# Moving the q and v steps of a blocked factorisation between its leaves, and the clearing of a tile behind one of them

## The chip, the cores and the metric

The kernel runs on one core of a Trainium2 chip. The metric is the time of one execution on the device in microseconds; the median of three runs of the kernel before is 1110.0 us (1108.01, 1110.0 and 1110.34).

## What is computed

A block of three layers on x of shape (8, 1024, 256), float32: half of a feed-forward with ternary weights, then an attention-like recurrence, then half of the same feed-forward. The recurrence is this, for each of 8 batches over 1024 tokens:

```
Q, K, V = x Wq' + bq, x Wk' + bk, x Wv' + bv          # H = 128
A = I, M = 0
for each token:  s = k.q ;  u = k / (|k| + eps)
                 Au = A u ;  denom = 1 + u.Au ;  A -= Au Au' / denom
                 M += v (s Au / denom)' ;  o = M q
```

The kernel does it in chunks of 128 tokens: 64 pairs of a chunk and a batch, each with a 128x128 matrix that is factorised. Q, V and the product of u and q (the s of every token) are needed only later.

## The kernel before, in words

Three phases follow each other, with a barrier of all engines between them: the first feed-forward with the keys; the **first factorisation**; and a third phase with a second factorisation, the outputs and the second feed-forward. The change touches the first factorisation alone (about 332 to 538.5 us in the trace). It gives the inverse factor T of every one of the 64 matrices, in the SBUF tile `T` of 128 x 64 x 128, and it makes q, v and u.q beside that.

The factorisation goes in four blocks of 32 rows, r = 0 to 3. VectorE's work of a block is `take(r)` (L1009, a transpose of the diagonal blocks out of PSUM), `leaf(r)` (L1018, L1021, L1033 and L1036: 32 dependent elimination steps on all 64 matrices at once) and `turn(r)` (L1046, L1047: transposes that publish the result on the semaphore `turned`). TensorE then does `finish_diagonal(r + 1)` in two halves of 128 matmuls of 32x32 each (L1268, then L1275); between them VectorE's `over_d(r)` (L1059) and ScalarE's `next_block(r)` copy what the second half reads. The second half lets `take(r + 1)` start. I call the stretch from the start of `turn(r)` to the start of `take(r + 1)` the turn-over r.

While VectorE is in leaf r, the other engines have the work that `beside(r)` lists: TensorE the products `done(r)` (L1195), `panel(r)` (L1202, L1215) and `diagonal(r + 1)` (L1202, L1255), ScalarE their copies, and between those the **steps of q and v**, sixteen in all (n = 0 to 15). A step is `qv(n)` on TensorE (L1286 for q, L1293 for v) and on ScalarE (L1152 and a copy), and on SyncE's DMA queue `store_q(n)` (L910), `load(n + 2)` (L897, the input tile of step n + 2, which may be asked for when TensorE is through with step n) and `store_v(n)` (L915). `QV_OF` says which steps go beside which leaf: 5, 4, 2 and 5.

u.q: `load_u(r)` (L905) brings the u of the steps of leaf r, VectorE multiplies them with q in `times_q(r)` behind `turn(r)` (L1078; at most three of them ahead of `over_d(r)`, the others behind it), and TensorE sums them in `dots(r)` (L1303), at the start of what it does beside leaf r + 1. `load_u(r)` waits for `dots(r - 1)`, since it reuses the buffers.

SyncE runs all DMAs of the phase on one queue, in program order: the weights, load(0), load(1), load_u(0), then **three DMAs that clear T's columns above the diagonal blocks** (L954: from zeros in `ident`, rows of 384, 256 and 128 bytes), and then for each r `keep_d` (L921), `load_u(r)`, `keep_rows(r - 1)` (L937, the finished rows into T) and the stores and loads of the steps of r.

TensorE waits in `qv(n)` until the input tile has landed (`a_in`), and it does `finish_diagonal(r + 1)` only when the steps beside leaf r are through, since they stand ahead of it in its program.

Of the kernel before, what the change touches and what calls it, by code (L numbers as in the profile page):

```python
# [32 lines left out]
NW = P // W  # L33
# [675 lines left out]

QV_OF = [range(0, 5), range(5, 9), range(9, 11), range(11, 16)]
QV_MAX = max(len(x) for x in QV_OF)

# [16 lines left out]
def factorise(nc, ctx, name, m, c, a=None):  # L732
# [16 lines left out]
    def sem(what):  # L749
        return ctx.enter_context(nc.semaphore(f"{name}_{what}"))  # L750
# [54 lines left out]
    if first:  # L805
        w_in = sem("wqv_in")
        a_in = [sem(f"aT_in{s}") for s in range(2)]
        u_in = sem("uT_in")
# [4 lines left out]
        uq_done = sem("uq_done")  # L813
        dots_done = sem("dots_done")
# [5 lines left out]
    def block_of(r):  # L820
        return slice(W * r, W * r + W)

    def rows_of(q):
        return slice(W * q, W * q + W)
# [7 lines left out]
    def after(r):  # L832

        return slice(W * (r + 1), P)
# [3 lines left out]
    def fills_of(r):  # L838
        out = []
        if r > 0:  # L840
            if first or r < NW - 1:
                out.append("done")
            if not first:
                out.append("done right")
        if r < NW:
            if first or r < NW - 1:
                out.append("panel")
            if not first:
                out.append("panel right")
        return out  # L850
# [32 lines left out]
    def slot(n):  # L883

        return next(n - x[0] for x in QV_OF if n in x)

    def beside(r):

        return zip_longest(fills_of(r), QV_OF[r] if first and r < NW else ())  # L890

    def sync(sp):
        def load(n):
            s = n % 2
            if n > 1:
                sp.wait_ge(v_made, n - 1)
            sp.dma_start(aT[s][:], m.aT[n]).then_inc(a_in[s], 16)  # L897

        def load_u(r):
            if r:  # L900

                sp.wait_ge(dots_done, r)
            for n in QV_OF[r]:
                half = slice(HC * (n % 2), HC * (n % 2) + HC)
                sp.dma_start(uT[:, slot(n)], uT_v[n // 2, :, half]).then_inc(u_in, 16)  # L905

        def store_q(n):
            half = slice(HC * (n % 2), HC * (n % 2) + HC)
            sp.wait_ge(q_done, n + 1)
            sp.dma_start(qT_v[n // 2, :, half], qT[:, slot(n)]).then_inc(q_stored, 16)  # L910

        def store_v(n):
            s = n % 2
            sp.wait_ge(v_done, n + 1)
            sp.dma_start(v_v[n // 2, :, HC * s:HC * s + HC], v_out[s][:]).then_inc(v_stored[s], 16)  # L915

        def keep_d(r):

            sp.wait_ge(turned, r + 1)
            for q in range(4):  # L920
                sp.dma_start(m.dinv[block_of(r), NQ * q:NQ * (q + 1)], dT[r][rows_of(q), 0:NQ]  # L921
                             ).then_inc(stored, 16)

        def keep_rows(r):

            what = "done" if first else "done right"
            sp.wait_ge(emptied, fill_number[r + 1, what] + 1)
            if r == NW - 1:
                sp.wait_ge(half_emptied, 1)
            if not first:  # L930

                sp.wait_ge(filled, fill_number[NW - 1, "panel right"] + 1)
            for q in range(4):
                pairs = slice(NQ * q, NQ * (q + 1))
                if first:
                    cols = slice(0, W * (r + 1))
                    sp.dma_start(m.T[block_of(r), pairs, cols], Y[r][rows_of(q), :, cols]  # L937
                                 ).then_inc(stored, 16)
                else:
                    sp.dma_start(m.W[block_of(r), pairs], YR[r][rows_of(q)]  # L940
                                 ).then_inc(e.rows_in[q] if r == NW - 1 else stored, 16)

        if first:
            w_v = a["WqkvT"].rearrange("(c p) n -> p c n", p=P)
            for i in range(2):
                sp.dma_start(wqv[:, :, i], w_v[:, :, 2 * i * H:(2 * i + 1) * H]).then_inc(w_in, 16)
            sp.dma_start(bq[:], a["bqkv"][0:H].rearrange("(p o) -> p o", o=1)).then_inc(w_in, 16)
            load(0)
            load(1)
            load_u(0)  # L950
            for i in range(NW - 1):

                zeros = c.ident[block_of(i), after(i)]
                sp.dma_start(m.T[block_of(i), :, after(i)],  # L954
                             zeros.unsqueeze(1).to_broadcast([W, NP, P - W * (i + 1)])).then_inc(stored, 16)

        def fetch_q():

            sp.wait_ge(diag_done, NW - 1)
            for g in range(4):  # L960
                pairs = slice(NQ * g, NQ * (g + 1))
                sp.dma_start(m.KK[:, pairs], m.qT[pairs].rearrange("n i j -> i n j")).then_inc(stored, 16)

        for r in range(NW + 1):
            if r:
                keep_d(r - 1)
                if first and r < NW:
                    load_u(r)
            if r == NW and e.early is not None:
                e.early(sp)  # L970
            if first and r:
                keep_rows(r - 1)
            if not first and r == NW - 1:
                fetch_q()
                for k in range(NW - 1):
                    keep_rows(k)
            if not first and r == NW:
                keep_rows(r - 1)
            if first and r < NW:
                for n in QV_OF[r]:  # L980
                    store_q(n)
                    if n + 2 < NSTEP:
                        load(n + 2)
                    store_v(n)
        if first:
            sp.wait_ge(q_stored, 16 * NSTEP)
            for s in range(2):
                sp.wait_ge(v_stored[s], 16 * NSTEP // 2)
        if e.early is None:
            sp.wait_ge(stored, e.all_stored)  # L990
            if not first:
                for q in range(4):
                    sp.wait_ge(e.rows_in[q], 16)

    def vector(v):
# [76 lines left out]

        def times_q(r, which):

            v.wait_ge(u_in, 16 * (QV_OF[r][-1] + 1))
            for n in which:
                v.wait_ge(q_done, n + 1)
                nc.vector.tensor_tensor(uT[:, slot(n)], uT[:, slot(n)], qT[:, slot(n)], ALU.mult  # L1078
                                        ).then_inc(uq_done, 1)

        for r in range(NW):
            take(r)
            leaf(r)
            turn(r)
            if r < NW - 1:
                if first:
                    times_q(r, QV_OF[r][:3])
                over_d(r)
                if first:
                    times_q(r, QV_OF[r][3:])  # L1090
            elif first:
                times_q(r, QV_OF[r])
        empty_half()

    def scalar(act):
        def copy(dst, src):
            return nc.scalar.activation(dst, src, ACT.Copy)
# [58 lines left out]
            copy(v_out[s][:], ps_v[:]).then_inc(v_done, 1)  # L1156

        def keep_dots():
            act.wait_ge(dots_done, NW)
            copy(dots_rows[:], ps_dots[0:NP, 0]).then_inc(rows_kept, 1)  # L1160
            act.wait_ge(rows_turned, 1)
            copy(m.uq[:], ps_dots[:, 1, 0:NP])
# [6 lines left out]
        for r in range(NW + 1):  # L1169
            if 0 < r < NW - 1:  # L1170
                act.wait_ge(turned, r)
                nc.scalar.mul(nd[:], dT[r - 1][:, 0:NQ], -1.0).then_inc(nd_done, 1)
                act.wait_ge(nd_done, r)
            for what, n in beside(r):
                if what is not None:
                    empty(r, what)
                if first and r == NW:
                    keep_dots()
                if n is not None:
                    qv(n)  # L1180
            if r < NW - 1:
                reset(r + 1)
                next_block(r)

    def tensor(pe):
# [110 lines left out]

        def dots(r):

            pe.wait_ge(uq_done, QV_OF[r][-1] + 1)
            for n in QV_OF[r]:  # L1300
                for j in range(HC):
                    at = n * HC + j
                    i = nc.tensor.matmul(ps_dots[0:NP, 0], c.ones_at[:, NP - 1 - at:2 * NP - 1 - at],  # L1303
                                         uT[:, slot(n), j], start=(at == 0), stop=(at == NP - 1))
            i.then_inc(dots_done, 1)
# [34 lines left out]
    if not first:  # L1340
        e.works, e.panels, e.Z, e.ZR, e.M, e.Tt = works, panels, Z, ZR, M, Tt
        e.inject_units = inject_units
    e.emptied, e.half_emptied, e.all_emptied = emptied, half_emptied, len(fill_list)
    e.sync, e.vector, e.scalar, e.tensor = sync, vector, scalar, tensor
    return e

# [660 lines left out]
```

## Time and profile before

| | |
|---|---|
| median of three runs | 1110.0 us |
| profiled execution, its own time | 1110.93 us |
| its span | 1109.2 us |
| TensorE busy | 933.6 us, 84% |
| VectorE busy | 798.4 us, 72% |
| ScalarE busy | 532.2 us, 48% |
| first factorisation, from take(0) to the start of the third phase | 334.1 to 538.5 us |
| mean DMA traffic | 103 GB/s |

The profile is of one execution. The page gives the busy time of each engine; the trace behind it gives every instruction with its start, its duration and what the engine waited for. A group of instructions is written as line, engine, operation, output and inputs, with how many there are; a square bracket gives the engine's idle time ahead of it and what ended it. "issue" in such a bracket means that nothing in the profile explains the wait. Rows marked PEld are weight loads, which stand ahead of each matmul.

### The profile page before, as it was taken

The page shows a single profiled execution, that of the slowest core. Times are in us where ns is not written, and L with a number is a line of the kernel's source. Part 1 is how long each engine was busy: PE and PEld are TensorE (multiplying, and loading weights), DVE is VectorE, ACT ScalarE, POOL GpSimd, SP SyncE. Part 2 cuts the span into 40 slices and gives each one's busy share as a digit, 9 for nine tenths or more (in the row PEclk, how much of TensorE's full clock was granted, in tenths as well). Part 3 has the DMA queues.
Part 4 walks back from the last instruction along what each step waited for, and adds up shares of the span by engine and source line. Part 5 has one row for each costly group of instructions (what it writes and reads, how often), then busy time and mean ns, then how long its engine had stood idle before and what let it go on. Part 6 is the DMA issues. An engine that isn't in the chain of part 4 may idle for free.

```text
span 1109.2 us, 28575 instructions
## 1 busy us (share of the span) xinstructions
PE 933.6 (84%) x11691; PEld 720.0 (65%) x11691; DVE 798.4 (72%) x2553; ACT 532.2 (48%) x1093; POOL 301.1 (27%) x256
## 2 busy tenths in 40 slices
PE   4799999999976796677899446692799999999998
PEld 1467777777763675565797425582667777777766
DVE  6878787877648898978359797886366666566663
ACT  4678787787741142112226212101165666556574
POOL 4355353535210000000000000000674554546340
PEclk9999999999997797889899776896899999999999
DMA  5353546455239452344443000056532433424231
GB/s 151 70 127 101 154 114 145 118 140 132 86 126 228 116 152 71 98 117 116 106 131 107 4 2 4 4 155 150 156 87 77 105 96 80 121 67 105 57 77 57
DMA packets 185522, 113.98 MB, mean 103 GB/s; under 512 B 85808, under 2 KB 178352, under 8 KB 184752
## 3 DMA queue, kind: packets, MB, share of 16 engines
q1 hardware_dynamic: 168496, 95.38, 33.9%
q10 hardware_dynamic: 16896, 16.78, 4.8%
q8 instruction: 92, 1.51, 0.6%
q14 instruction: 38, 0.31, 0.1%
HBM read 49.16 MB, written 37.75 MB: 78 GB/s over the span
## 4 chain that ended last, share of the span: by engine, by line
PE 33%; DVE 15%; issue 2%; POOL 1%; ACT 1%; DMA 0%; DVEq 0%; POOLq 0%; SPq 0%
PE ldl_work L1875 10%; PE ldl_work L1863 10%; DVE ldl_lane_matrix L1036 6%; DVE ldl_rank_one L1033 4%; DVE lane_rows L1018 2%; PE ldl_work L1847 2%; DVE ldl_lane_dinv L1021 2%; PE ldl_work L1439 2%; PE ldl_work L1449 1%; PE ldl_work L1817 1%; PE ldl_work L1830 1%; PE ldl_work L1831 1%; PE ldl_work L1838 1%; PE ldl_work L1195 1%; PE ldl_work L1811 1%
## 5 line engine op out<-in xcount | busy, mean ns | idle before, releaser
L1625 POOL TENSOR_TENSOR T<-T,out_bv_rows 128x512 f32<-128x512 f32 x16 | 20.4, 1272 | 453.9 <-DVE out_s_over_d L1728 448.0
L387 DVE TENSOR_TENSOR ffn_h_rest<-ffn_ps_h,ffn_h_high 128x512 f16<-128x512 f32 x128 | 87.2, 686 | 53.7 <-ACT ffn_ps_h L557 53.2
L556 ACT ACTIVATE ffn_h_high<-ffn_ps_h,b_columns 128x512 f16<-128x512 f32 x128 | 87.9, 686 | 65.4 <-PE ffn_ps_h L630 64.8
L1875 PE MATMUL ldl_work<-w_ternary,ldl_panels 128*128 128x256 f16 x512 | 118.2, 273 | 0.0
L644 PE MATMUL ffn_ps_y<-w_ternary,ffn_h_high 128*128 128x256 f16 x512 | 117.8, 273 | 0.0
L644 PE MATMUL ffn_ps_y<-w_ternary,ffn_h_rest 128*128 128x256 f16 x512 | 117.8, 272 | 0.0
L630 PE MATMUL ffn_ps_h<-ffn_xT_high,w_ternary 128*128 128x512 f16 x256 | 98.8, 386 | 11.2 <-DVE ffn_h_rest L387 11.0
L630 PE MATMUL ffn_ps_h<-ffn_xT_rest,w_ternary 128*128 128x512 f16 x256 | 98.6, 385 | 0.0
L1863 PE MATMUL ldl_work<-out_xT_high,w_ternary 128*128 128x512 f16 x256 | 97.0, 379 | 0.0
L1863 PE MATMUL ldl_work<-out_xT_rest,w_ternary 128*128 128x512 f16 x256 | 97.0, 379 | 0.0
L1776 ACT ACTIVATE ldl_work<-ldl_work,b_columns 128x512 f32<-128x512 f32 x128 | 84.0, 656 | 0.0
L557 ACT ACTIVATE ffn_ps_h<-ffn_ps_h,b_columns 128x512 f32<-128x512 f32 x128 | 83.9, 656 | 0.0
L1714 DVE TENSOR_TENSOR ldl_panels<-ldl_work,ldl_right_side 128x512 f16<-128x512 f32 x64 | 44.2, 691 | 50.6 <-ACT ldl_work L1776 50.2
L1714 DVE TENSOR_TENSOR ldl_panels<-ldl_work,ldl_panel 128x512 f16<-128x512 f32 x64 | 44.2, 691 | 49.4 <-ACT ldl_work L1776 49.1
L1775 ACT ACTIVATE ldl_right_side<-ldl_work,b_columns 128x512 f16<-128x512 f32 x64 | 44.0, 688 | 55.9 <-PE ldl_work L1863 55.3
L1775 ACT ACTIVATE ldl_panel<-ldl_work,b_columns 128x512 f16<-128x512 f32 x64 | 44.1, 689 | 54.9 <-PE ldl_work L1863 54.5
L1036 DVE SCALAR_TENSOR_TENSOR inv_lane_matrix<-inv_rank_one,inv_lane_dinv,inv_lane_matrix 128x480 f32<-128x480 f32 (+15 forms) x124 | 61.3, 495 | 4.4
L1036 DVE SCALAR_TENSOR_TENSOR ldl_lane_matrix<-ldl_rank_one,ldl_lane_dinv,ldl_lane_matrix 128x480 f32<-128x480 f32 (+15 forms) x124 | 61.3, 494 | 4.4
L644 PEld LDWEIGHTS ffn_ps_y<-w_ternary,ffn_h_rest 128*128 128x128 f16 x512 | 50.1, 98 | 17.0
L1875 PEld LDWEIGHTS ldl_work<-w_ternary,ldl_panels 128*128 128x128 f16 x512 | 50.1, 98 | 17.0
L644 PEld LDWEIGHTS ffn_ps_y<-w_ternary,ffn_h_high 128*128 128x128 f16 x512 | 50.1, 98 | 16.9
L1875 PE MATMUL ldl_work<-w_ternary,ldl_panel 128*128 128x256 f16 x256 | 59.3, 273 | 0.0
(216 smaller groups left out, 2295.9 us busy)
## 6 DMA issues: line engine op xcount, KB each, us to landing
ffn_x<-in_x SPq DMA_DIRECT2D x16, 512.0 KB, 4.7
x_scratch<-ffn_x_out ACTq DMA_DIRECT2D x16, 512.0 KB, 3.3
aT_scratch<-ffn_aT SPq DMA_DIRECT2D x16, 512.0 KB, 5.3
inv_aT<-aT_scratch SPq DMA_DIRECT2D x16, 512.0 KB, 4.9
ldl_panels<-uT_scratch SPq DMA_DIRECT2D x32, 256.0 KB, 3.0
T<-x_scratch SPq DMA_DIRECT2D x16, 512.0 KB, 3.8
uT_scratch<-ffn_uT SPq DMA_DIRECT2D x16, 256.0 KB, 5.4
inv_uT<-uT_scratch SPq DMA_DIRECT2D x16, 256.0 KB, 4.3
```

Of the source, the lines that this page charges most:

```text
L387: nc.vector.tensor_tensor(hl[n % 2][:, f], ps_h[f % 3][:], hh[n % 2][:, f], ALU.subtract).then_inc(hl_done, 1)
L556: nc.scalar.activation(hh[n % 2][:, f], ps_h[f % 3][:], ACT.Gelu, bias=c.b1[:, f:f + 1])
L557: nc.scalar.activation(ps_h[f % 3][:], ps_h[f % 3][:], ACT.Gelu, bias=c.b1[:, f:f + 1]).then_inc(g_done, 1)
L630: ins = nc.tensor.matmul(ps_h[f % 3][:], c.w1[:, d, f * P:(f + 1) * P], part[s][:, :, d], start=(k == 0), stop=(k == 2 * DC - 1))
L644: ins = nc.tensor.matmul(ps_y[t % 2][:], part[n % 2][:, f, t * P:(t + 1) * P], c.w2[:, f], start=(f == 0 and part is hh), stop=(f == FC - ...
L1033: note(nc.vector.tensor_tensor(prod[:, :n], M[:, r0:, j:j + 1].to_broadcast(shape), R[:, j:j + 1, window].to_broadcast(shape), ALU.mult))
L1036: i = nc.vector.scalar_tensor_tensor(out=M[:, r0:, window], in0=prod[:, :n], scalar=dl[:, j:j + 1], in1=M[:, r0:, window], op0=ALU.mult, o ...
L1714: nc.vector.tensor_tensor(hl[k % 2][:, f], ps_h[f % 3], hh[k % 2][:, f], ALU.subtract).then_inc(hl_done, 1)
L1775: nc.scalar.activation(hh[k % 2][:, f], ps_h[f % 3], ACT.Gelu, bias=c.b1[:, f:f + 1])
L1776: nc.scalar.activation(ps_h[f % 3], ps_h[f % 3], ACT.Gelu, bias=c.b1[:, f:f + 1]).then_inc(g_done, 1)
L1863: ins = nc.tensor.matmul(ps_h[f % 3], c.w1[:, d, f * P:(f + 1) * P], part[s][:, :, d], start=(j == 0), stop=(j == 2 * DC - 1))
L1875: ins = nc.tensor.matmul(ps_y[t % 2], part[k % 2][:, f, t * P:(t + 1) * P], c.w2[:, f], start=(f == 0 and part is hh), stop=(f == FC - 1 a ...
```

## The change

The steps beside the leaves become 7, 4, 0 and 5. T's upper columns are cleared in a function of its own, which SyncE runs behind the first step's `store_v` beside the second leaf (n = 7). The waits for u, for the products and for the sums are written so that a leaf without steps is left out. The buffers for u and q hold seven steps where they held five.

```diff
-QV_OF = [range(0, 5), range(5, 9), range(9, 11), range(11, 16)]
+QV_OF = [range(0, 7), range(7, 11), range(11, 11), range(11, 16)]
...
         def load_u(r):
-            if r:
+            if r and QV_OF[r]:
-                sp.wait_ge(dots_done, r)
+                sp.wait_ge(dots_done, sum(1 for y in QV_OF[:r] if y))
...
             load(0)
             load(1)
             load_u(0)
+
+        def clear():
             for i in range(NW - 1):
                 zeros = c.ident[block_of(i), after(i)]
                 sp.dma_start(m.T[block_of(i), :, after(i)],
                              zeros.unsqueeze(1).to_broadcast([W, NP, P - W * (i + 1)])).then_inc(stored, 16)
...
                     store_v(n)
+                    if n == QV_OF[1][0]:
+                        clear()
...
-            v.wait_ge(u_in, 16 * (QV_OF[r][-1] + 1))
+            v.wait_ge(u_in, 16 * QV_OF[r].stop)
...
-            act.wait_ge(dots_done, NW)
+            act.wait_ge(dots_done, sum(1 for y in QV_OF if y))
...
         def dots(r):
-            pe.wait_ge(uq_done, QV_OF[r][-1] + 1)
+            if not QV_OF[r]:
+                return
+            pe.wait_ge(uq_done, QV_OF[r].stop)
```

## Rows read from the trace of the kernel before

**Rows 1.** Windows of the first and last leaf, VectorE: stretch, length, busy, clock, DMA.

```profile
334.08:375.30 41.22, 37.63 (x159) 0.79 0.89 224
...
480.56:521.80 41.24, 37.65 (x159) 0.99 0.57 155
```

**Rows 2.** Timeline of VectorE, turn-over 0: start, duration, line, operation, idle before.

```profile
376.56 1.86 DVE L1078 TENSOR_TENSOR inv_uT<-inv_uT,inv_qT 128x512 f32<-128x512 f32 x3
378.99 0.76 DVE L1059 SCALAR_TENSOR_TENSOR inv_panel_over_d<-inv_work,inv_dinv_turned 128x256 f32<-128x256 f32 x2 [0.57 <-PE inv_work L1268]
379.67 1.28 DVE L1078 TENSOR_TENSOR inv_uT<-inv_uT,inv_qT 128x512 f32<-128x512 f32 x2
381.92 0.72 DVE L1009 STREAM_TRANSPOSE inv_lane_matrix<-inv_work 128x512 f32<-128x512 f32 x1 [0.97 <-PE inv_work L1275]
```

**Rows 3.** Timeline of VectorE, both ends of turn-over 1.

```profile
423.16 1.25 DVE L1046 STREAM_TRANSPOSE inv_T_turned<-lane_rows 128x1024 f32<-128x1024 f32 x1
...
429.83 0.72 DVE L1009 STREAM_TRANSPOSE inv_lane_matrix<-inv_work 128x512 f32<-128x512 f32 x1 [1.57 <-PE inv_work L1275]
```

**Rows 4.** Timeline of VectorE, both ends of turn-over 2.

```profile
471.05 1.25 DVE L1046 STREAM_TRANSPOSE inv_T_turned<-lane_rows 128x1024 f32<-128x1024 f32 x1
...
480.56 0.72 DVE L1009 STREAM_TRANSPOSE inv_lane_matrix<-inv_work 128x512 f32<-128x512 f32 x1 [2.75 <-PE inv_work L1275]
```

**Rows 5.** Timeline of TensorE: steps of q and v, finish_diagonal and dots.

```profile
355.79 3.78 PE L1286 MATMUL inv_ps_q<-inv_aT,inv_wqv 128*128 128x512 f32 x4 [7.96 <-DMA inv_aT<-aT_scratch]
359.36 3.15 PE L1293 MATMUL inv_ps_v<-inv_wqv,inv_aT 128*128 128x128 f32 x16
...
376.78 2.04 PE L1268 MATMUL inv_work<-inv_panel,inv_T_turned 32*32 32x32 f32 x128 [6.75 <-DVE inv_dinv_turned L1047]
...
381.76 6.52 PE L1303 MATMUL inv_ps_dots<-inv_uT,ones_at 128*64 128x128 f32 x40
...
414.77 1.95 PE L1293 MATMUL inv_ps_v<-inv_wqv,inv_aT 128*128 128x128 f32 x16
424.64 2.04 PE L1268 MATMUL inv_work<-inv_panel,inv_T_turned 32*32 32x32 f32 x128 [7.93 <-DVE inv_dinv_turned L1047]
...
504.64 1.88 PE L1286 MATMUL inv_ps_q<-inv_aT,inv_wqv 128*128 128x512 f32 x4
...
513.42 1.98 PE L1286 MATMUL inv_ps_q<-inv_aT,inv_wqv 128*128 128x512 f32 x4 [0.78 <-DMA inv_aT<-aT_scratch]
```

**Rows 6.** Timeline of SyncE's DMA issues: start, time the queue took, count.

```profile
338.84 9.83 SPq L954 DMA_DIRECT2D T<-ident  x3
...
350.22 0.51 SPq L897 DMA_DIRECT2D inv_aT<-aT_scratch  x1
...
397.25 2.67 SPq L937 DMA_DIRECT2D T<-inv_panel_done  x4
...
401.17 0.46 SPq L915 DMA_DIRECT2D v_scratch<-inv_v  x1
...
482.80 2.56 SPq L905 DMA_DIRECT2D inv_uT<-uT_scratch  x5
```

**Rows 7.** Windows: PE, PEld, DVE, ACT, POOL busy, clock, DMA share, GB/s.

```profile
335.00:341.30 6.30, 5.93 (x38) 2.18 (x39) 5.89 (x19) 1.73 (x5) 0.00 (x0) 0.76 1.05 323
...
341.30:351.20 9.90, 6.54 (x69) 5.07 (x67) 9.23 (x31) 2.88 (x5) 0.00 (x0) 1.00 1.12 185
...
351.60:361.90 10.30, 6.11 (x16) 4.04 (x17) 9.48 (x38) 0.69 (x1) 0.00 (x0) 0.50 0.70 216
```

**Rows 8.** Timeline of TensorE from diagonal(3) into turn-over 2.

```profile
462.32 2.49 PE L1255 MATMUL inv_work<-inv_panel_done,inv_panel_over_d 32*32 32x32 f32 x221
467.76 0.79 PE L1255 MATMUL inv_work<-inv_panel_done,inv_panel_over_d 32*32 32x32 f32 x35 [2.95 <-issue]
472.53 1.57 PE L1268 MATMUL inv_work<-inv_panel,inv_T_turned 32*32 32x32 f32 x92 [3.98 <-DVE inv_dinv_turned L1047]
476.10 0.78 PE L1268 MATMUL inv_work<-inv_panel,inv_T_turned 32*32 32x32 f32 x36 [2.00 <-issue]
```

**Rows 9.** DMA of 467.8 to 473.2 us, all queues.

```profile
DMA packets 0, 0.00 MB, mean 0 GB/s; under 512 B 0, under 2 KB 0, under 8 KB 0
```

**Rows 10.** DMA of 473.2 to 476.1 us: queue, packets, MB, share.

```profile
q8 instruction: 1, 0.02, 2.6%
```

## The prediction

> **What bounds the kernel now.** I read the windows of the four leaves first. A leaf takes VectorE 41.2 us, the first [rows 1] as the last, whether DMA moves 224 GB/s beside it or 155, and VectorE is busy for 37.6 of it; the two between are alike. So the first factorisation is four leaves that nothing beside them slows, and what lies between: three turn-overs and an end. Work beside a leaf costs nothing as long as it is through when the leaf is. Next comes VectorE's timeline at the turn-overs. Turn-over 1 takes 429.83 - 423.16 = 6.67 us [rows 3], turn-over 2 takes 480.56 - 471.05 = 9.51 us [rows 4]. Both end with a wait for TensorE's L1275. The chain in each is turn, L1268 on TensorE, over_d, L1275, take. Only in these stretches, or by keeping TensorE from starting L1268 when `turned` comes, can the change move the time. TensorE's slack ahead of L1268 is 6.75 us behind leaf 0, 7.93 behind leaf 1 [rows 5] and 3.98 behind leaf 2 [rows 8]. The extra 2.84 us of turn-over 2 is mostly on TensorE: L1268 runs 92 of its matmuls, stands still for 2.00 us with "issue" as the cause and runs 36 more [rows 8].
>
> *Leaf 0, seven steps and seven loads of u; no clearing ahead of them.* In before, the three clearing DMAs held SyncE's queue for 9.83 us, from 338.84, so step 2's tile was asked for at 350.22 [rows 6] and TensorE waited 7.96 us for it, until 355.79 [rows 5]. Without them load_u takes two more issues and step 2 can start near 349. The four steps of leaf 3 that follow closely take (513.42 - 504.64)/2 = 4.39 us each [rows 5]; five more steps at that pace end at 349 + 5 x 4.4 = 371, which leaves 5 us before L1268 at 376.8. Nothing is paid. If each step took 1.1 us more, this cover would be gone.
>
> *Turn-over 0.* times_q(0) has seven multiplications, three ahead of over_d as now and four behind it where there were two. Three take 1.86 us, so one takes 0.61 [rows 2]. The four start at 379.67 and end near 382.1; take(1), which started at 381.92 after 0.97 us of idleness, starts then: **+0.2 us** (bounds 0 and +0.5).
>
> *dots(0)* sums seven steps. Forty matmuls for five take 6.52 us [rows 5], 1.30 a step: +2.6, and it starts 0.3 later since it waits for the last multiplication. Everything that TensorE does beside leaf 1, and what follows from it on ScalarE and SyncE, is late by **3.0 us**; leaf 1's slack of 7.93 hides that.
>
> *The clearing in leaf 1.* The queue's order there is keep_rows(0), store_q(7), load(9), store_v(7), clear, store_q(8), **load(10)**, store_v(8). Step 10 is the last beside leaf 1, and TensorE has to do it before L1268. In before, the first store_v of the leaf ended at 401.17 + 0.46 = 401.6 [rows 6]; now at 404.6, where the clearing starts. In before its tile was usable 355.79 - 338.84 = 16.95 us after the clearing's start. That distance carries over, since what stands between them is the same: three clearings, a store of q, a load. In it the clearing itself takes 9.9 us of DMA at 185 GB/s [rows 7]. The queue is somewhat fuller this time (keep_rows, q, tile and v ahead of it); I add 0.6. Step 10's tile is there at 404.6 + 16.95 + 0.6 = **422.2 us**. Its price depends on the clock. TensorE will have been idle from about 415.6 (step 9, which in before was step 7, ended 3 us before the leaf's last) to 422.2. After its 7.96 us of idleness in before the granted clock was 0.50, the lower level of 1.2 GHz [rows 7], and the step took 359.36 + 3.15 - 355.79 = 6.72 us; at the full clock it is 1.98 + 1.95, less an overlap, 3.8 [rows 5]. So it ends between 426.0 and 428.9. L1268 would start at 424.64 + 0.2. The delay lies between 1.2 and 4.1 us for that landing, and between 0 and 5 when the landing is moved by 1 to 2 us as well. I take **+3.6**, near the upper end, since the idle time ahead is near to the one that cost the clock; 0.2 more for a fetch of instructions that now falls into DMA traffic (0 to 1). Who waits: VectorE's over_d and take(2) and ScalarE's reset of the lane matrix, all behind L1268, so all of it is on the path.
>
> *Leaf 2 without steps.* TensorE loses two steps, 7.8 us, but diagonal(3) then waits for ScalarE to empty the panel, so it ends only a little earlier against its leaf; it had 3.98 us of slack and needed none of it. VectorE loses two multiplications that lay in a wait of 3.49 us for L1268. dots(2) is gone. None of that is on the path. load_u(3) comes at about 476 instead of 482.80 [rows 6], ahead of keep_rows as before; nobody waits for it before leaf 3's end.
>
> *Turn-over 2's stall.* Up to L1268 of turn-over 2 TensorE has run the same eleven steps, and two steps of dots more, 16 matmuls or 32 instructions. The edges of the blocks fall 16 matmuls earlier against the program: 51 ahead of the end of L1255, and 76 into L1268. TensorE has then run about 102 instructions of the new block before it goes into the wait for `turned`, where it had run 70. Turn-overs 0 and 1 each follow a wait of 7 to 8 us and have an edge in L1268 too, and neither stalls (2.04 us for 128 matmuls, [rows 5]). So I take it that the next block is asked for in time: turn-over 2 falls from 9.51 to 6.67, **-2.84 us** (bounds -2.84 and 0).
>
> *Leaf 3 and the end.* The five steps are the same, dots(2)'s 2.4 us are gone ahead of them, the slack there grows. The three clearings are waited for only at the end of the phase. No instruction of the third phase moves. Nothing.
>
> **Sum.** +0.2 + 3.6 + 0.2 - 2.84 = +1.2 us. The profiled execution took 1110.93 us for its span of 1109.2, 0.93 above the median of the runs; so 1112.1 against it and **1111.2** against the median of 1110.0. About 0.2% of this kernel, 2.2 us, is what a measurement can tell from no change.
>
> **The rivals.** *(A) The forecast*, 1111.2, between 1109.6 and 1112.6: 0.42.
>
> *(B) The stall stays.* Against me speaks that I know only that the fetch was late in that place, not why; TensorE goes on waiting on `turned` shortly after a block's edge as before. Then the late step is paid in full with nothing against it: 1110.0 + 0.2 + 3.6 + 0.2 = 1114.0. This ends on the slower side. Its place is TensorE's program ahead of L1268 of turn-over 1, its price 3.8 us, and it decides as soon as step 10's tile lands after 424.8 - 3.8 = 421.0 us. 0.33.
>
> *(C) The clearing is through earlier, or the clock holds, and the stall goes.* The loads of u moved 323 GB/s [rows 7]; the clearing's 1.57 MB would take 4.9 us at that rate instead of 9.9, step 10's tile would be there at 417.2, TensorE would have hardly been idle, and step 10 would end at 421. Then only +0.2 - 2.84 is left: 1107.4. For it: in leaf 0 the clearing shared the queue with a backlog of u; against it: it is the same DMA, and the 185 GB/s were moved with the engines at a share of 1.12. 0.10. (The Trainium skill, DMA: Bandwidth & Descriptors, section Why small descriptors are slow, says that transfers from SBUF to SBUF don't suffer the penalty of small descriptors. The trace disagrees: 185 GB/s for rows of 128 to 384 bytes against 323. By the page it would be this rival.)
>
> *(D) Both*: the tile comes in time and the stall stays, 1110.2: 0.10.
>
> *(E) The steps of leaf 0 don't fit*, or a fetch stall turns up in turn-over 0 or 1: 1113 or more, 0.05.
>
> **How the numbers follow.** Slower by over 0.2% is above 1112.2: B, E, and 0.05 of A: 0.43. Faster is below 1107.8: C and 0.03 of A: 0.13. Within: 0.44. The range takes in B and C's ends: 1107.4 to 1114.9 (B with a landing 1 us later). The likeliest case's own range is 1109.6 to 1112.6.
>
> **What would show it.** The clearing starts near 404.6 on SyncE's queue; TensorE waits about 6 us for an input tile at step 10, with a granted clock of 0.50, and L1268 of turn-over 1 starts near 428 with next to no idle time ahead of it, or one ended by TensorE itself; turn-over 1 takes about 10.5 us and turn-over 2 about 6.7. Turn-over 0 takes 6.8. If L1268 of turn-over 1 still waits for `turned`, my landing is wrong; if turn-over 2 still has an "issue" of 2 us in L1268, the -2.84 is. The leaves must stay at 41.2. If one doesn't, the whole ground is wrong.

## The result and the profile after

The changed kernel takes 1117.16 us in the median of 12 runs (1113.96 to 1119.75), the kernel before 1110.36 in 12 runs beside it (1108.01 to 1113.33). The ratio is 1.0055, with a 95% interval of 1.0043 to 1.0066: **slower**, by about 6 us. I had 1111.2 within 1107.4 to 1114.9; the median lies above the range.

The profiled execution took 1115.08 us. The page's span and busy times, of the changed kernel:

```profile
span 1113.3 us, 28573 instructions
## 1 busy us (share of the span) xinstructions
PE 935.2 (84%) x11691; PEld 721.9 (65%) x11691; DVE 798.1 (72%) x2553; ACT 532.4 (48%) x1093; POOL 301.0 (27%) x256
```

The engines have nearly the work of before: TensorE 1.6 us more, the others less than 0.3. The rest of the loss is in waits. In the changed file L1268 and L1275 are L1272 and L1279, L1286 and L1293 are L1290 and L1297, L1046 is L1050, L1009 is L1013. VectorE's timeline, both ends of each turn-over (start, duration, line, operation, idle before):

```profile
374.30 1.25 DVE L1050 STREAM_TRANSPOSE inv_T_turned<-lane_rows 128x1024 f32<-128x1024 f32 x1
...
382.55 0.72 DVE L1013 STREAM_TRANSPOSE inv_lane_matrix<-inv_work 128x512 f32<-128x512 f32 x1 [1.39 <-PE inv_work L1279]
...
423.77 1.25 DVE L1050 STREAM_TRANSPOSE inv_T_turned<-lane_rows 128x1024 f32<-128x1024 f32 x1
...
434.83 0.72 DVE L1013 STREAM_TRANSPOSE inv_lane_matrix<-inv_work 128x512 f32<-128x512 f32 x1 [3.42 <-PE inv_work L1279]
...
476.05 1.25 DVE L1050 STREAM_TRANSPOSE inv_T_turned<-lane_rows 128x1024 f32<-128x1024 f32 x1
...
483.15 0.72 DVE L1013 STREAM_TRANSPOSE inv_lane_matrix<-inv_work 128x512 f32<-128x512 f32 x1 [2.62 <-PE inv_work L1279]
```

The leaves between are 41.2 us as before [rows 1]. The turn-overs are 8.25, 11.06 and 7.10 us where they were 6.62, 6.67 [rows 3] and 9.51 [rows 4]: +1.63, +4.39 and -2.41. Turn-over 1 on TensorE:

```profile
422.24 3.78 PE L1290 MATMUL inv_ps_q<-inv_aT,inv_wqv 128*128 128x512 f32 x4 [7.89 <-DMA inv_aT<-aT_scratch]
425.81 2.12 PE L1297 MATMUL inv_ps_v<-inv_wqv,inv_aT 128*128 128x128 f32 x16
427.86 2.02 PE L1272 MATMUL inv_work<-inv_panel,inv_T_turned 32*32 32x32 f32 x128
430.96 0.59 PE L1279 MATMUL inv_work<-inv_panel_done,inv_panel_over_d 32*32 32x32 f32 x46 [1.07 <-ACT inv_panel_done L1101]
433.47 1.33 PE L1279 MATMUL inv_work<-inv_panel_done,inv_panel_over_d 32*32 32x32 f32 x82 [1.92 <-issue]
```

Step 10 starts at 422.24, after 7.89 us of waiting for its input tile, and L1272 follows without a gap: TensorE, not `turned`, is the last to come. Then L1279 stands still for 1.92 us after 46 matmuls. SyncE's queue in the same stretch:

```profile
404.32 10.94 SPq L956 DMA_DIRECT2D T<-ident  x3
415.30 2.38 SPq L910 DMA_DIRECT2D qT_scratch<-inv_qT  x1
417.73 0.50 SPq L897 DMA_DIRECT2D inv_aT<-aT_scratch  x1
```

Step 10's tile is the last of these rows, behind the clearing and a store. Turn-over 0 has a new stall of 1.35 us, five matmuls ahead of the end of L1279, and turn-over 2 has lost its own: L1272's 128 matmuls run in one piece.

```profile
378.90 1.93 PE L1279 MATMUL inv_work<-inv_panel_done,inv_panel_over_d 32*32 32x32 f32 x123 [1.07 <-ACT inv_panel_done L1101]
382.18 0.32 PE L1279 MATMUL inv_work<-inv_panel_done,inv_panel_over_d 32*32 32x32 f32 x5 [1.35 <-issue]
...
468.23 0.72 PE L1259 MATMUL inv_work<-inv_panel_done,inv_panel_over_d 32*32 32x32 f32 x51 [0.99 <-issue]
477.54 2.04 PE L1272 MATMUL inv_work<-inv_panel,inv_T_turned 32*32 32x32 f32 x128 [8.59 <-DVE inv_dinv_turned L1051]
```

### The profile page after: what moved, and what is told of

Read it like the earlier page. It is cut to its first block, busy times and chain, and to the rows that moved or that the text cites. A ratio compares the mean times of both kernels' runs of the same rounds, so it can differ in the third digit from the quotient of the medians.

```text
span 1113.3 us, 28573 instructions
## 1 busy us (share of the span) xinstructions
PE 935.2 (84%) x11691; PEld 721.9 (65%) x11691; DVE 798.1 (72%) x2553; ACT 532.4 (48%) x1093; POOL 301.0 (27%) x256
## 4 chain that ended last, share of the span: by engine, by line
PE 33%; DVE 15%; issue 2%; ACT 1%; DMA 0%; POOL 0%; DVEq 0%; SPq 0%; ACTq 0%
PE ldl_work L1881 10%; PE ldl_work L1869 10%; DVE ldl_lane_matrix L1040 6%; DVE ldl_rank_one L1037 4%; PE ldl_work L1853 2%; DVE lane_rows L1022 2%; DVE ldl_lane_dinv L1025 2%; PE ldl_work L1445 2%; PE ldl_work L1823 1%; PE ldl_work L1844 1%; PE ldl_work L1836 1%; PE ldl_work L1455 1%; PE ldl_work L1837 1%; PE ldl_work L1817 1%; PE ldl_work L1272 1%
```

## The experiments

All times are medians, and each ratio is to the kernel before on the same chip in the same batch (there it took 1110.2 us in two batches, and 1111.0 beside the kernels "a step later" and "256 more"). The turn-overs are of the one profiled execution of each kernel, read as above.

That execution isn't always a typical one. That of the steps alone was the fastest of its nine (1111.61 us, median 1115.8), so its turn-overs explain only part of the median. That of the kernel before with 40 instructions more was the slowest of its twelve (1113.87 us): its turn-overs are short and its first factorisation ended 5.9 us earlier than before, but 579.5 us followed it where 570.6 do in the kernel before. That excess isn't explained; the three other kernels with the 40 instructions have 570.6 to 571.8 there.

| kernel | turn-overs 0, 1, 2 (us) | median (us) | ratio to before, 95% interval |
|---|---|---|---|
| before | 6.62, 6.67, 9.51 | 1110.4 | |
| changed, first profile | 8.25, 11.06, 7.10 | 1117.2 | 1.0055 (1.0043 to 1.0066) |
| changed, second profile | 10.77, 12.06, 7.09 | 1116.9, one run | |
| steps only | 11.95, 7.18, 7.11 | 1115.8 | 1.0041 (1.0028 to 1.0054) |
| clearing only | 6.63, 11.01, 9.50 | 1114.0 | 1.0031 (1.0020 to 1.0042) |
| clearing beside leaf 2 | 10.05, 6.67, 8.43 | 1112.3 | 1.0009 (0.9999 to 1.0019) |
| larger buffers only | 6.84, 6.67, 10.06 | 1110.4 | 0.9992 (0.9980 to 1.0004) |
| changed, 40 instructions more | 6.77, 10.59, 7.08 | 1111.4 | 1.0005 (0.9994 to 1.0016) |
| the same, clearing a step later | 6.77, 8.25, 6.77 | 1110.3 | 1.0007 (0.9986 to 1.0028) |
| clearing beside leaf 2, 40 more | 6.85, 6.63, 6.75 | 1108.8 | 0.9984 (0.9971 to 0.9997) |
| before, 40 more | 6.73, 6.94, 6.69 | 1107.7 | 0.9977 (0.9963 to 0.9992) |
| before, 256 more | 6.62, 6.85, 9.24 | 1110.7 | 0.9998 (0.9987 to 1.0009) |

**The steps alone.** My theory was that turn-over 1's loss is the tile behind the clearing; the rival, that it is where TensorE's blocks of instructions fall.

```diff
-                    if n == QV_OF[1][0]:
-                        clear()
...
+        if first:
+            clear()
         for r in range(NW + 1):
```

> The steps are 7, 4, 0, 5 as in the changed kernel, but the three clearing DMAs stand ahead of leaf 0's stores as in the kernel before. Theory (the price of turn-over 1 is step 10's input tile behind the clearing): step 10 of leaf 1 is in time, so turn-over 1 loses the wait of 3.2 us for TensorE and takes 6.7 to 8.6 us instead of 11.06. The price moves to leaf 0: step 2 starts at about 356 at the half clock, five steps of 4.4 us end near 380, so L1268 of turn-over 0 starts 3 to 4 us late and turn-over 0 takes 10 to 12 us. Time near that of the changed kernel. Rival (the price is in where the blocks of instructions fall, not in the clearing): turn-over 1 stays near 11 us and turn-over 0 near 8.2.

Turn-over 1 fell to 7.18 and the loss moved to turn-over 0, 11.95 us. There the last step beside leaf 0 ended at 379.8, and L1272 followed with no gap, 4.1 us behind the turn-over's start where it was 1.5; that is 2.6 us of the 5.3 that turn-over 0 grew. Another 2.2 us are two stalls with "issue" as the cause, 0.43 in L1272 and 1.77 in L1279. So the late step follows the clearing, and about half of the loss is it. The seven steps fit beside leaf 0 only because the clearing has left it.

**The clearing alone.**

```diff
-QV_OF = [range(0, 7), range(7, 11), range(11, 11), range(11, 16)]
+QV_OF = [range(0, 5), range(5, 9), range(9, 11), range(11, 16)]
```

> The steps are 5, 4, 2, 5 as before; only the clearing is moved, behind the first store_v beside leaf 1 (n = 5). Theory: the last step beside leaf 1 (now step 8) waits for its tile until about 419 to 420 us and runs at the half clock; it ends at 423 to 427, so turn-over 1 grows by 0 to 2 us, from 6.67 to 7 to 9. TensorE's blocks of instructions fall as in the kernel before, so turn-over 0 stays at 6.6 and turn-over 2 near 9.5. Time +0 to +2 us. Rival (block positions alone made the loss): no difference to the kernel before beyond that.

It costs more than I expected, +4.34 us in turn-over 1 and 3.8 in the median. The timeline of TensorE shows the two parts, the last step late and then a stall of 1.60 us:

```profile
421.26 3.78 PE L1290 MATMUL inv_ps_q<-inv_aT,inv_wqv 128*128 128x512 f32 x4 [7.49 <-DMA inv_aT<-aT_scratch]
424.83 2.82 PE L1297 MATMUL inv_ps_v<-inv_wqv,inv_aT 128*128 128x128 f32 x16
...
433.54 0.55 PE L1279 MATMUL inv_work<-inv_panel_done,inv_panel_over_d 32*32 32x32 f32 x25 [1.60 <-issue]
```

Turn-overs 0 and 2 are those of the kernel before, the second with its stall.

**The clearing beside leaf 2**, where no step waits behind it.

```diff
-                    if n == QV_OF[1][0]:
-                        clear()
...
             if first and r:
                 keep_rows(r - 1)
+            if first and r == 2:
+                clear()
```

> The steps are 7, 4, 0, 5, and the clearing stands beside leaf 2, behind keep_rows(1), where SyncE has no step to serve. Theory: no step waits for a tile behind the clearing; turn-over 1 takes 6.7 to 8.6 us (with or without the stall in L1279), turn-over 2 stays at 7.1, turn-over 0 at 8.2. The first factorisation is then 3 to 5 us shorter than in the changed kernel, and the time 0 to 2 us under that of the kernel before. Rival: if the loss comes from block positions and the clock, the time stays near 1116.

Turn-over 1 is 6.67 again and the median falls by 4.9 us. But turn-over 0 took 10.05, which I had not expected, and the time is no better than before.

The changed kernel, the one with the steps alone and this one have the same program on TensorE, so its blocks have the same edges. At the edge behind 46 matmuls of L1279 in turn-over 1 the changed kernel stood still for 1.92 us. First the same place with the clearing beside leaf 0, then with the clearing beside leaf 2:

```profile
434.71 1.33 PE L1279 MATMUL inv_work<-inv_panel_done,inv_panel_over_d 32*32 32x32 f32 x82 [0.35 <-issue]
```

```profile
430.89 2.04 PE L1279 MATMUL inv_work<-inv_panel_done,inv_panel_over_d 32*32 32x32 f32 x128 [1.07 <-ACT inv_panel_done L1101]
```

Without the clearing beside leaf 1 the stall there is 0.35 us or none. So 1.6 to 1.9 us of turn-over 1's loss come with the clearing as well, beside the late step.

**The buffers alone.** The first profile of the changed kernel also had 3 us more behind the first factorisation, where nothing was changed.

```diff
-QV_MAX = max(len(x) for x in QV_OF)
+QV_MAX = 7
```

> The kernel before with the buffers of u and q made for seven steps instead of five; nothing else. If the tiles' places in SBUF have a price, it shows here: the changed kernel lost 1.25 us in the Gram products and 2.0 us behind the second factorisation, 3 us in all. I expect no difference, within 1.5 us of the kernel before; the rival (placement) expects +3.

No difference. The tiles' places have no price. The second profile of the changed kernel had the same time behind the first factorisation as the kernel before (570.6 us in both), so those 3 us belonged to one execution.

**A second profile of the changed kernel**, to see whether turn-over 0 repeats.

> The changed kernel as it is, a second look. In the first, the next block was fetched 0.01 us before TensorE went into the wait of turn-over 0, and the turn-over took 8.25 us; in the kernel with the clearing beside leaf 2 it was not, and it took 10.05. If that is a race, the second look may show 10.0; turn-over 1 near 11 in either case.

It doesn't. It took 10.77 us, with two stalls:

```profile
376.94 2.04 PE L1272 MATMUL inv_work<-inv_panel,inv_T_turned 32*32 32x32 f32 x123 [7.46 <-DVE inv_dinv_turned L1051]
380.80 0.33 PE L1272 MATMUL inv_work<-inv_panel,inv_T_turned 32*32 32x32 f32 x5 [1.81 <-issue]
382.16 1.93 PE L1279 MATMUL inv_work<-inv_panel_done,inv_panel_over_d 32*32 32x32 f32 x123 [1.04 <-ACT inv_panel_done L1101]
385.86 0.32 PE L1279 MATMUL inv_work<-inv_panel_done,inv_panel_over_d 32*32 32x32 f32 x5 [1.77 <-issue]
```

Both stalls fall after 123 matmuls, one block of 256 instructions apart. The edge before them therefore fell 4 matmuls ahead of the end of step 6's v product, 0.3 to 0.4 us before TensorE went into the wait for `turned`. The DMA packets of that wait and of the start of the turn-over, 369.2 to 376.8 and then 376.8 to 380.8 us (queue: packets, MB, share):

```profile
DMA packets 1519, 1.25 MB, mean 165 GB/s; under 512 B 67, under 2 KB 1377, under 8 KB 1519
...
q1 hardware_dynamic: 1519, 1.25, 58.0%
...
q8 instruction: 1, 0.02, 2.3%
```

All 1519 packets of the wait are data; TensorE's next block comes only when the wait is over. In the first profile it came at the last moment, while TensorE was going into the wait (DMA of 369.5 to 375.6 us):

```profile
q8 instruction: 1, 0.02, 1.0%
```

and L1272 ran through; the stall of 1.35 us at the next edge was left. That is the fetch of [rows 8 to 10], in a new place: an edge shortly ahead of a wait, and the next block is not fetched until the wait ends. It looks like a race, won in the first profile and lost in the second. The kernel with the clearing beside leaf 2 has the same program up to here and lost it too (10.05 us, stalls of 1.37 and 1.49). The second profile's time is also the one near the median.

**Forty instructions more.** This tests that directly: the rest of the program is the same, and its edges move by 40 instructions.

```diff
+PAD = 20
...
             if first and r == 0:
+                for _ in range(PAD):
+                    nc.tensor.matmul(ps_q[:, 0], c.ident16[:], c.ident16[:], start=True, stop=True)
                 pe.wait_ge(w_in, 48)
```

In the kernel with the clearing beside leaf 2:

> Steps 7, 4, 0, 5 and the clearing beside leaf 2, and besides 20 matmuls of 128x128 float16 into the free PSUM tile of q, ahead of panel(0): 40 instructions that compute nothing and move the edges of TensorE's blocks of 256 instructions against the program. Without them the wait for `turned` of turn-over 0 begins 8 instructions behind an edge, 0.44 us, and the next block is then asked for only after the wait (10.05 us, with stalls of 1.37 and 1.49). Theory (an edge shortly ahead of a wait defers the fetch): with them the wait begins 48 instructions behind the edge, several us later, so turn-over 0 takes 6.8 to 7.0, turn-over 1 6.7, turn-over 2 7.0 to 8.4. Time 2 us under the kernel before, 1107.5 to 1109, and 3 to 4 under the same kernel without the 20 matmuls (1112.3). Rival (the stalls are chance, or come from the seven multiplications or the DMA traffic of seven steps): turn-over 0 stays at 8 to 10 us and the time at 1112.

In the kernel before:

> The kernel before with the same 20 matmuls ahead of panel(0) and nothing else. The wait for `turned` of turn-over 2, which began 70 instructions and 0.56 us behind an edge, begins 110 behind it. Theory: turn-over 2 loses its stall and takes 6.7 to 7.5 us instead of 9.5 with its two steps still beside leaf 2; turn-overs 0 and 1 stay at 6.6 to 6.7; time 1107.5 to 1108.5, so the gain that the change had in turn-over 2 didn't need the move of the steps. Rival (turn-over 2 was long since TensorE has too much to do beside leaf 2): it stays at 9.5 and the time at 1110.

In the changed kernel:

> The changed kernel with the same 20 matmuls. Theory: turn-over 0 falls to 6.8 to 7.0; turn-over 1 keeps the late step (3.2 us of wait for TensorE) and stays between 9.5 and 11; turn-over 2 at 7. Time 1.5 to 3 us under the changed kernel, about 1113 to 1115. Rival (the late step is a matter of instruction fetch): turn-over 1 falls to 6.7.

And the control, 128 smaller matmuls, a whole block of 256 instructions, in the kernel before:

```diff
-PAD = 20
+PAD = 128
...
-                    nc.tensor.matmul(ps_q[:, 0], c.ident16[:], c.ident16[:], start=True, stop=True)
+                    nc.tensor.matmul(ps_q[0:W, 0, 0:W], c.ident16[0:W, 0:W], c.ident16[0:W, 0:W], start=True, stop=True)
```

> A control: the kernel before with 128 matmuls of 32x32 float16 ahead of panel(0), 256 instructions, one whole block, so that every edge falls where it falls in the kernel before. Theory (position alone counts): turn-over 2 keeps its stall, 9.5 to 10 us, turn-overs 0 and 1 stay at 6.6 to 6.7, and the time stays at 1110 within 1 us. Rival (any extra work for TensorE at the start helps, by the clock or the pace of the steps): turn-over 2 falls to 6.7 and the time to 1107.7 as with 40 instructions.

All four came out the theory's way, with small misses: the changed kernel took 1111.4 where I had 1113 to 1115, turn-over 2 took 9.24 in the control where I had 9.5 to 10, and 6.75 with the clearing beside leaf 2 where I had 7.0 to 8.4, and turn-over 1 of the kernel before 6.94 and 6.85 where I had 6.6 to 6.7. By the ratios, forty useless instructions take 2.6 us off the kernel before, 2.8 off the one with the clearing beside leaf 2 and 5.5 off the changed one; 256 take nothing off. TensorE in turn-over 2, first of the kernel before with 40 more, then with 256 more:

```profile
468.40 1.06 PE L1256 MATMUL inv_work<-inv_panel_done,inv_panel_over_d 32*32 32x32 f32 x55 [2.73 <-issue]
472.34 2.05 PE L1269 MATMUL inv_work<-inv_panel,inv_T_turned 32*32 32x32 f32 x128 [2.87 <-DVE inv_dinv_turned L1048]
```

```profile
468.41 0.53 PE L1256 MATMUL inv_work<-inv_panel_done,inv_panel_over_d 32*32 32x32 f32 x35 [2.97 <-issue]
473.01 1.57 PE L1269 MATMUL inv_work<-inv_panel,inv_T_turned 32*32 32x32 f32 x92 [4.08 <-DVE inv_dinv_turned L1048]
476.58 0.78 PE L1269 MATMUL inv_work<-inv_panel,inv_T_turned 32*32 32x32 f32 x36 [2.00 <-issue]
```

With 40, 55 matmuls follow the edge instead of 35, the wait begins later behind it, and L1269 runs in one piece. The next block's packet came during the wait this time (one packet on q8 between 469.2 and 472.3 us). With 256 the row of 92, the stall of 2.00 us and the row of 36 are those of [rows 8] to the hundredth.

**The clearing a step later**, in the changed kernel with the 40 instructions, so that load(10) stands ahead of it.

```diff
-                    if n == QV_OF[1][0]:
+                    if n == QV_OF[1][1]:
```

> The changed kernel with the 20 matmuls, and the clearing one step later: behind the second step's store_v beside leaf 1 (n = 8) instead of the first's. load(10) is then ahead of the clearing on SyncE's queue, and nothing else is changed. Theory (the price of turn-over 1 is that the last step's tile stands behind the clearing in the queue): turn-over 1 falls from 10.59 to 6.7 to 7.5 us although the clearing's traffic still runs beside leaf 1; time as with the clearing beside leaf 2, 1108 to 1109.5. Rival (the traffic as such, or the fuller queue ahead of the turn-over, is what costs): turn-over 1 stays above 9 us and the time at 1111.

Turn-over 1 fell by 2.3 us, to 8.25, not to 7.5 as I had it. Step 10 is in time; the rest is a stall. This kernel and the one with the clearing beside leaf 2 and 40 more have the same program on TensorE. First this one in turn-over 1 with its window (PE, PEld, DVE, ACT, POOL busy, clock, DMA share, GB/s), then the other:

```profile
425.23 2.04 PE L1273 MATMUL inv_work<-inv_panel,inv_T_turned 32*32 32x32 f32 x128 [6.53 <-DVE inv_dinv_turned L1052]
428.34 0.62 PE L1280 MATMUL inv_work<-inv_panel_done,inv_panel_over_d 32*32 32x32 f32 x26 [1.07 <-ACT inv_panel_done L1102]
430.30 1.60 PE L1280 MATMUL inv_work<-inv_panel_done,inv_panel_over_d 32*32 32x32 f32 x102 [1.34 <-issue]
...
424.00:432.00 8.00, 4.35 (x257) 4.07 (x258) 4.23 (x9) 1.50 (x4) 0.00 (x0) 0.50 0.88 263
```

```profile
424.89 2.05 PE L1273 MATMUL inv_work<-inv_panel,inv_T_turned 32*32 32x32 f32 x128 [7.43 <-DVE inv_dinv_turned L1052]
428.01 1.93 PE L1280 MATMUL inv_work<-inv_panel_done,inv_panel_over_d 32*32 32x32 f32 x128 [1.07 <-ACT inv_panel_done L1102]
...
424.00:432.00 8.00, 6.04 (x266) 5.89 (x267) 5.73 (x14) 1.50 (x4) 0.00 (x0) 0.50 0.03 6
```

The granted clock is 0.50 in both. With 263 GB/s of stores and loads held up by the clearing, L1280 stalls for 1.34 us at an edge; with 6 GB/s it doesn't. The packet with TensorE's next block shows where that comes from. Here none had started by 427.9 us, 2.7 us behind the start of L1273 (DMA of 425.2 to 427.9 us, then of 427.9 to 430.3); in the other kernel one came between 425.9 and 428.0, at 426.0, 1.1 us behind it.

```profile
q1 hardware_dynamic: 537, 0.69, 94.9%
...
q1 hardware_dynamic: 1076, 0.82, 107.0%
q8 instruction: 1, 0.02, 2.3%
```

So the clearing beside leaf 1 has two prices: the tile behind it, 2.3 us here, and the queue's traffic pushed into the turn-over, 1.6 us. They don't simply add up. With the tile late, L1273 started 5.33 us behind the turn-over's start and not 1.48, 3.85 later, but then the traffic was 192 GB/s (428.6 to 433.7 us) and not 300 (425.2 to 431.9 us), the granted clock 1.00 and not 0.50, and the stall only 0.44 us; that left 2.3.

## Why the prediction was wrong, point by point

- **Leaf 0 takes seven steps**: right. I had the last one end near 371; it ended at 370.2. In the kernel with the steps alone they didn't fit, as the 5 us of cover suggested.
- **Turn-over 0, +0.2 us**: wrong, and the largest miss. It is +1.6 in one profile and +4.15 in the other. The multiplications cost what I said: in the three kernels with seven steps and the 40 instructions, turn-over 0 is 6.77 to 6.85, +0.15 to +0.23. What I put at nothing is the fetch of TensorE's program there: two more steps ahead of turn-over 0, 40 matmuls or 80 instructions, move its edges as well (in turn-over 1 it is these and the two more of dots). I worked out that move for turn-over 2 alone, where it gained, and gave a fetch stall in turn-overs 0 and 1 a chance of 0.05 in rival E, together with another case. The forecast called both turn-overs safe for having no stall in the kernel before, which is true only of the old positions.
- **Step 10's tile at 422.2 us**: right, 422.24. The step cost 5.7 us, between my 3.8 and 6.7, at a mean granted clock of 0.65 and not the 0.50 that I expected, and L1272 started 427.86 - 423.77 = 4.09 us behind the turn-over's start where it was 424.64 - 423.16 = 1.48 [rows 3, 5]: 2.6 us late, against my 3.6 (3.8 in the second profile). The wait of 7.89 us for the tile came as described, longer than my 6.6 since step 9 ended at 414.34 and not at 415.6.
- **A later fetch in turn-over 1, +0.2 (0 to 1)**: the right mechanism, mis-sized; the 0.2 was a guess from no row. The stall was 1.92 us and 1.83 in the second profile. With the same program on TensorE it is 0.35 or nothing when the clearing is not beside leaf 1, and the clearing a step later shows why: the traffic behind it delays the fetch, for a stall of 1.3 us there.
- **The rival of a cheaper clearing** didn't happen: it held the queue for 10.94 us, and 9.83 before [rows 6]. The Trainium skill, DMA: Bandwidth & Descriptors, section Why small descriptors are slow, says that transfers within SBUF don't suffer from small descriptors. The trace of the changed kernel doesn't bear that out: the clearing's packets of 384 and 256 bytes took 26 and 27 ns (medians), as long as the 27 of the loads' and stores' packets of 512. Whether it is the packet's size alone isn't shown, since the clearing also writes only 32 partitions at a time.
- **Turn-over 2, -2.84 us**: right in mechanism and nearly in size, -2.41. It is a gain of where the edges fall and not of the steps' place: the kernel before with 40 instructions more has 6.69 with its two steps still beside leaf 2. Moving the steps off leaf 2 gains nothing by itself.
- **The sum.** In the second profile, which has the median's time, it is +4.15 + 5.39 - 2.42 = +7.1 in the turn-overs. The end behind leaf 3 was 1.2 us shorter, which leaves +5.9 up to the third phase and +6.0 for the execution (1116.92 against 1110.93). My sum lacked 3.95 in turn-over 0 and 1.6 in turn-over 1, took 0.4 too much off turn-over 2, and had nothing for the end behind leaf 3. The failed step is thus the one that took turn-overs 0 and 1 as safe from fetch stalls.

What stays open: why the wait holds back the fetch. The runs show that it does when an edge falls 8 or 70 instructions ahead of the wait, not which part of the chip decides it. It isn't the time alone: 70 instructions (0.34 to 0.56 us from the first matmul behind the edge to the last) deferred the fetch, and 102 instructions in 0.53 us, turn-over 2 of the changed kernel, did not. How the 12 runs of the changed kernel divide between races won and lost can't be told, since only two were profiled. The length of the end behind leaf 3 varies too, 13.9 to 16.7 us over the profiled kernels and 1.2 us between the kernel before and its copy with 256 instructions more, which isn't explained.

## What to carry to other kernels

When TensorE's chain between two phases is hundreds of tiny matmuls, count its instructions from one stall to the next; if they are 256 apart, any edit of its program moves the stalls, and a change must be judged with the edges shifted as well, by some tens of useless instructions in a slack place. Here the edit won nothing beyond that in any form: with 40 of them its best form, the clearing beside leaf 2, has a ratio of 0.9984 and the kernel before 0.9977, and the two intervals overlap. A long run of small transfers belongs on a queue's stretch where nothing behind it is waited for before the next turn-over, and its held-up traffic must be through by then too.

## What the runs showed of the hardware that I had not expected

An edge of a block of 256 TensorE instructions that falls 8 or 70 instructions ahead of a semaphore wait (0.3 to 0.6 us) can defer the next fetch until the wait is over, though the wait lasts 3.1 to 7.5 us; the cost is 1.4 to 2.3 us at the next edge, and in turn-over 0 as much again at the one behind it (1.49 to 1.77). It repeats: turn-over 2 took 9.2 to 10.1 us in all four kernels in which the wait began 70 instructions behind the edge, and 6.7 to 7.1 in seven of the eight profiles in which it began 102 or more behind (8.43 in the one with the clearing beside leaf 2 and no padding, where TensorE came to the wait only 1.1 us before its end). In turn-over 0, 8 instructions behind the edge, one profile of three escaped. The Trainium skill, Runtime: NRT & Kernel Launch, section Instruction fetch mechanics, gives blocks of 256 instructions, as the traces do, and calls the crossing of an edge mostly hidden. In the first factorisation of the kernel before 25 blocks were fetched and TensorE stood still 8 times with "issue" as the cause, 12.0 us in all, so most edges were hidden and some were dear: a block of 32x32 matmuls runs in 2.0 us, and at these stalls TensorE went on 2.2 to 2.7 us after the packet with the next block had started. Busy queues add to it: at 263 GB/s an edge cost 1.34 us that cost nothing at 6 GB/s.
